# Moving the first batch's last stage into the second batch's attention, in one freed accumulation bank

## The reference

```python
def _L1_attn_ref(x, Wq, Wk, Wv, Wo, W_down_kv, W_up_k, W_up_v):
    ...
            scores = jnp.einsum('bhqd,bhkd->bhqk', qh, kh) * scale
            ...
            scores = scores * decay[None, None, :, :]
            ...
            attn = jax.nn.softmax(scores, axis=-1)
            out = jnp.einsum('bhqk,bhkd->bhqd', attn, vh)
            out = out.transpose(0, 2, 1, 3).reshape(B, S, D_MODEL)
            return (out @ Wo, latent_kv)
    ...
def _L1_ffn_ref(x, base_w, base_b, gate_w, lora_A, lora_B):
    ...
        logits = jnp.einsum('td,ed->te', xf, gate_w)
        probs = jax.nn.softmax(logits, axis=-1)
        weights, selected = jax.lax.top_k(probs, TOP_K)
        ...
        z = jnp.einsum('td,erd->ter', xf, lora_A)
        moe = jnp.einsum('ter,te,eor->to', z, ew, lora_B) * SCALING
        base = jnp.einsum('td,od->to', xf, base_w) + base_b
        out = (base + moe).reshape(x.shape[:-1] + (D_OUT,))
...
    x = x + _L1_attn_ref(_layernorm(x, axis=-1), L1_attn_Wq, ...)
    x = x + 0.5 * _L1_ffn_ref(_layernorm(x, axis=-1), L1_ffn_base_w, ...)
    return x
```

## Time and profile before

| | |
|---|---|
| median of 3 runs | 791.61 us (789.17 to 791.88) |
| the profiled execution | 787.95 us, its span 786.1 us |
| PE, DVE, ACT, POOL busy | 86%, 61%, 71%, 34% of the span |
| attention's exponentials | 466.8 to 728.2 us of the span |
| after the last exponential | 58.0 us |

### The profile page before, as it was taken

The page is one execution under the profiler, slowest core; times in us unless marked ns, Lnnn a source line. Parts: engine busy times, 40 slices in busy tenths (PEclk is TensorE's granted clock), DMA queues, the critical chain, the costliest instruction groups (busy, mean ns, idle before and its releaser), DMA issues.

```text
span 786.1 us, 11233 instructions
## 1 busy us (share of the span) xinstructions
PE 679.1 (86%) x3617; PEld 399.5 (51%) x3617; DVE 482.3 (61%) x1258; ACT 557.4 (71%) x789; POOL 271.2 (34%) x298
## 2 busy tenths in 40 slices
PE   3789788878889899999777769999999999999587
PEld 2566566656566667777555532332323223232364
DVE  4789877878798778988856552344322223222474
ACT  4657574666767666655453569999999999999243
POOL 3286456665667556455620430112000000000110
PEclk9999999999999999999958689999999999999858
DMA  9002232323223223333200189100199100000001
GB/s 261 11 1 70 80 97 80 90 84 91 86 82 97 90 84 115 102 124 114 73 15 0 27 179 194 31 1 1 20 187 196 29 1 1 1 1 1 3 1 54
DMA packets 31343, 54.55 MB, mean 69 GB/s; under 512 B 4624, under 2 KB 13280, under 8 KB 29776
## 3 DMA queue, kind: packets, MB, share of 16 engines
q1 hardware_dynamic: 30128, 53.38, 26.3%
q0 software_dynamic: 224, 0.34, 0.2%
q10 hardware_dynamic: 928, 0.06, 0.1%
HBM read 35.71 MB, written 1.28 MB: 47 GB/s over the span
## 4 chain that ended last, share of the span: by engine, by line
PE 33%; ACT 31%; issue 14%; DVE 13%; POOL 7%; ACTq 0%; DVEq 0%; POOLq 0%
ACT raw_w L836 26%; PE bank L1421 7%; PE bank L1423 6%; PE bank L1422 6%; POOL act_parts L576 4%; PE bank L1546 2%; PE bank L1543 2%; PE bank L1544 2%; PE bank L1461 2%; DVE act L1094 2%; DVE bank L1083 1%; POOL rstd L523 1%; DVE up L1072 1%; ACT xt L665 1%; PE bank L1476 1%
## 5 line engine op out<-in xcount | busy, mean ns | idle before, releaser
L836 ACT ACTIVATE raw_w<-bank,minus_c 128x1024 f32<-128x1024 f32 x256 | 259.6, 1165 | 1.8 <-PE bank L1722 0.7
L576 POOL TENSOR_TENSOR act_parts<-act,act_parts 128x512 fp32r<-128x512 f32 x128 | 167.4, 1309 | 120.6 <-ACT act_parts L737 99.9
L1266 DVE TENSOR_TENSOR bank<-bank,fix 128x256 f32<-128x256 f32 x128 | 55.3, 433 | 177.9 <-PE bank L1699 177.9
L723 ACT ACTIVATE bank<-bank,b_gate 128x512 f32<-128x512 f32 x112 | 74.1, 662 | 113.9 <-PE bank L1423 64.4
L1421 PE MATMUL bank<-xn_parts,w_hi 128*128 128x512 f32 x256 | 109.6, 428 | 20.1 <-ACT bank L723 10.2
L1072 DVE TENSOR_SCALAR up<-bank,b_up 128x512 f32<-128x512 f32 x128 | 95.5, 746 | 36.0 <-PE bank L1423 32.3
L1423 PE MATMUL bank<-xn_parts,w_hi 128*128 128x512 f32 x256 | 102.7, 401 | 0.0
L1422 PE MATMUL bank<-xn_parts,w_lo 128*128 128x512 f32 x256 | 102.4, 400 | 0.0
L520 POOL TENSOR_SCALAR var_eps<-mean_var 128x4 f32<-128x4 f32 x28 | 7.4, 263 | 236.2 <-DVE mean_var L940 234.9
L1094 DVE SCALAR_TENSOR_TENSOR act<-up,bank 128x512 f32<-128x512 f32 x128 | 86.6, 676 | 0.0
L737 ACT ACTIVATE act_parts<-act 128x512 fp32r<-128x512 f32 x128 | 79.8, 623 | 4.2 <-DVE act L1094 4.2
(11 more groups left out here) (204 smaller groups left out, 1057.6 us busy)
## 6 DMA issues: line engine op xcount, KB each, us to landing
grow<-scores SPq DMA_DIRECT2D x68, 256.0 KB, 3.2
early<-scores SPq DMA_DIRECT2D x44, 256.0 KB, 3.2
raw_w<-in_gate_up SPq DMA_DIRECT2D x4, 512.0 KB, 8.8
w_lo<-gelu_parts SPq DMA_DIRECT2D x8, 256.0 KB, 5.1
w_lo<-act_parts SPq DMA_DIRECT2D x8, 256.0 KB, 5.5
w_hi<-gelu_parts SPq DMA_DIRECT2D x6, 256.0 KB, 4.7
w_hi<-act_parts SPq DMA_DIRECT2D x6, 256.0 KB, 5.5
x_tok<-in_x SPq DMA_DIRECT2D x4, 256.0 KB, 4.4
```

The costliest lines, as they stand in the source:

```text
L576: pool.tensor_tensor(act_lo[:, j % NACT, :], act[:, j % NACT, :], act_hi[:, j % NACT, :].bitcast(F32), ALU.subtract).then_inc(s["lo_ready" ...
L723: eng.activation(out, bank[:, G, :], ACT.Gelu_apprx_sigmoid, bias=b_gate[:, e:e + 1]).then_inc(s["glu_ready"], 1)
L836: eng.activation(probs[:, u % NP, :], pair, ACT.Exp, bias=minus_c[:, b:b + 1])\
```

## The change

A table `EARLY` lays the whole remainder of chunks 0 and 1 (heads, projection, low-rank layer, turning back) into the steps of the second batch's attention: on PE at odd steps t from 69 to 125, behind `scores(2t + 1)`; on DVE at units u from 141 to 252, behind that unit's `fix_scores`. Of these chunks' work only the small router exponential stays on ACT (ahead of the exponentials of u = 190 and 201); the splits, scaled rows and copies that ACT did for all chunks are done by DVE for chunks 0 and 1. The stage "ffn1b" behind the attention begins with chunk 2 (`first=QC`).

The banks: from sum 8 on, all sums accumulate in bank 6 alone, so the first `weigh` of a sum waits until DVE has copied the sum before out; `take_out` moves from the sixth unit of the next sum to the fourth, `normalize` from the fourteenth to the tenth, `turn` from its sixth step to its fourth. Everything else (the turned sums and all 20 early steps of PE) shares bank 7, one after the other: `early_free` makes each wait for the reader of the one before.

```diff
+EARLY = {
+    "pe": {69: ("heads", 0), 71: ("heads", 1), 73: ("out", 0), 77: ("out", 1), 79: ("t1", 0), 85: ("t2", 0), 87: ("t1", 1),
...
+    "act": {190: ("exp", 0), 201: ("exp", 1)},
+}
...
+        def o_bank(n):
+
+            return 6 + n % 2 if n < G4 * QC else 6
...
+        turn_after = {KB // 2 * G4 * QC * 2 + KB * i + 3: ("turned", G4 * QC + i - 1) for i in range(G4 * QC)}
...
+                    if u in EARLY["act"]:
+                        router_exp(3, EARLY["act"][u][1])
...
-                    if u % (2 * KB) == 5 and n > 0:
+                    if u % (2 * KB) == (5 if u < UNITS else 3) and n > 0:
                         take_out(n - 1)
-                    if u % (2 * KB) == 13 and n > 0:
+                    if u % (2 * KB) == (13 if u < UNITS else 9) and n > 0:
                         normalize(n - 1)
+                    if u in EARLY["dve"]:
+                        early_step(*EARLY["dve"][u])
...
                     if i == 0 and n >= 2:
-                        pe.wait_ge(s["normed"], n - 1)
+                        pe.wait_ge(s["normed"], n - 1 if n <= G4 * QC else G4 * QC - 1)
+                    if i == 0 and n > G4 * QC:
+                        pe.wait_ge(s["ot_copied"], n)
...
-                    if t % KB == 5 and t >= KB:
+                    if t % KB == 5 and KB <= t < UNITS // 2:
                         turn(t // KB - 1)
+                    if t in turn_after:
+                        early_free("turned", turn_after[t][1])
+                        turn(turn_after[t][1])
+                    if t in EARLY["pe"]:
+                        name, c = EARLY["pe"][t]
+                        early_free(name, c)
+                        if name == "heads":
+                            pe.wait_ge(s["normed"], heads_whole(c))
+                        early_step(name, c)
...
+            def early_free(name, i):
+
+                at = early_uses.index((name, i)) if name != "last" else len(early_uses)
+                if at >= 1:
+                    signal, value = early_read(*early_uses[at - 1])
+                    pe.wait_ge(s[signal], value)
...
-            skewed("ffn1b", "pe", {**lora(LN_FFN1B, 3, X_ATTN), "turn": turn_back})
+            skewed("ffn1b", "pe", {**lora(LN_FFN1B, 3, X_ATTN), "turn": turn_back}, first=QC)
```

More of the change, by code:

```diff
@@ L360, in side, with skewed @@
                             chains[chain][name](c)
-        def skewed(phase, engine, ops, once={}):
+        def skewed(phase, engine, ops, once={}, first=0):
             stage, order = STAGES[phase], ORDERS[phase][engine]
-            for step in range(NC + max(stage.values())):
+            for step in range(first, NC + max(stage.values())):
                 if step in once:
@@ L369, in skewed @@
                 for name in order:
-                    if 0 <= step - stage[name] < NC:
+                    if first <= step - stage[name] < NC:
                         ops[name](step - stage[name])
@@ L856, in attention @@
                     attn_fast()
-                    for b in range(NB):
-                        attn_heads(b)
+                    attn_heads(1)
                 with eng.Else():
@@ L918, in _ @@
             attention()
-            skewed("ffn1b", "act", {**lora(LN_FFN1B, 3), "copy": out_copy})
+            skewed("ffn1b", "act", {**lora(LN_FFN1B, 3), "copy": out_copy}, first=QC)
         @block.vector
@@ new lines, in early_hi, with early_score_copy @@
+            def early_hi(c):
+                eng.wait_ge(s["t2_ready"], norm_at(LN_FFN1B, c) + 1)
+                eng.tensor_copy(xn_hi[:, chunk(c)], bank[:, t2_bank(LN_FFN1B, c), :]).then_inc(s["xn_hi_ready"], 1)
+            def early_score_copy(c):
+                eng.wait_ge(s["score_psum_ready"], 3 * NC + c + 1)
+                for g in range(G4):
+                    eng.wait_ge(s[f"stack{g}_loaded"], stacks_in(g, 1))
+                eng.tensor_copy(score_rows_of(3, c), bank[0:2 * TRUE1, scores_bank(3, c), :])\
+                    .then_inc(s["score_ready"], 1)
@@ L1357, in attn_out @@
                 for c in range(QC * b, QC * (b + 1)):
[L1358 to L1360 removed]
+                    attn_add(c)
             def attention():
@@ L1413, in _ @@
             attention()
-            skewed("ffn1b", "dve", lora(LN_FFN1B, 3))
+            skewed("ffn1b", "dve", lora(LN_FFN1B, 3), first=QC)
         @block.tensor
@@ L1729, in turn @@
                     for t in range(TPC):
-                        last = pe.transpose(bank[:, 6 + n % 2, 128 * t:128 * (t + 1)],
+                        last = pe.transpose(bank[:, turned_bank(n), 128 * t:128 * (t + 1)],
                                             out_t[:, n % 2, 128 * t:128 * (t + 1)], ident[:])
@@ L1796, in attention @@
                     pe.wait_ge(s["ao_ready"], 1)
-                    for c in range(NC):
+                    before = None
+                    for name, c in EARLY["pe"].values():
+                        if before:
+                            signal, value = early_read(*before)
+                            pe.wait_ge(s[signal], value)
+                        early_step(name, c)
+                        before = name, c
+                    for c in range(QC, NC):
                         head_in(c)
-                for b in range(NB):
-                    attn_out(b)
+                attn_out(1)
             pe.wait_ge(s["ident_loaded"], 16)
```

181 lines of the change are left out of this document (133 added, 48 removed).

## The result

The changed kernel takes **780.61 us** in the median of 4 runs (778.69 to 781.08), the kernel before, run beside it, 791.71 us (789.17 to 791.88). The ratio is 0.986, with a 95% interval from 0.984 to 0.989: some 11 us faster, where 4.5 were forecast. The profiled execution took 781.08 us, its span is 779.2 us. Two later rounds gave 0.989 (0.981 to 0.997) and 0.987 (0.984 to 0.990).

A forecast was written before the change was run, and what follows sets the result against it. ACT bounds the second batch's attention, chains the tail behind it. Attention +10.4 us (9.1 pieces, 0.4 router exponentials, 0.9 bank and `logits(1)`), tail -14.9, net -4.5: profiled execution 783.5, median 787.1 us; range 783 to 792.

The forecast's parts named there:

- What bounds the kernel: Second batch's attention: ACT full, 32.88 of 33.00 us; behind the attention no engine full, chains set the pace, mean clock 0.70.
- The slack of 0.30: Second batch's attention: `turn` takes 0.59 us of PE and ACT loses 0.29, so PE has 0.30 us free per inserted piece.
- I price it as its time on PE less 0.30: Early PE pieces in the second batch's attention: each costs ACT that much, 4.55 us a chunk, 9.1 for two.
- lower bound of 6 us: Second batch's attention: least growth, if half of each piece's price is made up for; 10.4 us was the forecast.
- The single bank: First `weigh` of sums 9, 11, 13, 15 waits for the copy: 0.5 us each, partly filled by early pieces, 0.8 in all.
- `logits(1)`'s wait: Second batch's attention: `logits(1)` waits for its split, 0.1 us.
- The router exponentials: Two small exponentials on the full ACT in the second batch's attention: 0.2 us each, 0.4 together.
- DVE's work at nothing: Second batch's attention: DVE's added 28 us for both chunks cost no time, since DVE is busy only 9.09 of 33 us.
- Rival 2: Attention: early DVE pieces wait for PE and delay corrections at ten places; at 1 us each 797.1 us, slower; chance 0.10.
- What the tail gives back: From the last exponential to the end: 43.15 us instead of 58.0, 14.9 less, walked step by step at half clock.
- Rival 3: Tail: the clock returns to full from `zs(3)` on, 2.3 us more gain, 784.8 us; chance 0.15.
- aside on another price for the transposes: Skill page's 56 ns per product: an insert of four costs about 0.07 us, ten of them 2.2 us less than forecast.

The follow-up runs named there:

- doubled transposes: Kernel before with `turn` at step 6, its four transposes done twice in a row there; against single transposes there, both batches' exponentials span 265.9 us, +6.7.
- half of the change: Changed kernel with the single accumulation bank and only chunk 0's steps early, chunk 1's left behind the attention; 787.2 us, 0.994 of the kernel before.
- single-bank kernel: Kernel before with every second-batch sum accumulating in bank 6 and turned into bank 7, no early pieces; second batch's exponentials span 131.3 us, before 129.1.

## Why the prediction was wrong, and where it was right

**What bounds the kernel** was right: ACT in the attention, chains behind it.

**The slack of 0.30** was right for a lone piece: `logits(1)` lost 0.67 of 1.00, the doubled transposes 0.73 of 1.02.

**The step that failed is "I price it as its time on PE less 0.30", for each of the 20 pieces by itself.** They stand two steps apart for the most part, and there the slack is 0.30 plus what the piece two steps ahead has cost. Priced by that rule, with the prediction's own times on PE (and 1.0 for `logits`), the steps from 67 to 125 give: `turn` 0.29, heads 0 and 0.29, projection 0.20, `turn` 0.09, projection 0.40, `t1` 0, `turn` 0.29, `t2` 0, and so on, 6.9 us in all with the turns. Measured were stalls of 7.5 us over the whole stretch. Of these 0.24 are the two router exponentials, 0.07 the bank, and 0.28 a delay on ACT ahead of one exponential (below); 6.9 are left. The turns alone had cost 2.34 before, so the pieces added 4.6 us, where the prediction had 9.1. The rule is not exact at single places: it gives 0.29 and then 0.20 for `scores(0)` and `z(0)`, and 0.04 and 0.51 were measured; `back(0)` cost 0.88 instead of 0.70. The errors cancel in the sum, and that they do so nearly exactly is in part luck.

The prediction's lower bound of 6 us, "if half of each piece's price is made up for", was the right idea without the reason, and even so too high.

**The single bank** was sized rightly, wait and cost (0.5 against 0.45, 0.8 in all against 0.7 alone). In the changed kernel it cost 0.07 in sum 11, and at sums 9, 13 and 15 nothing that can be told from the pieces there: here too the coupling takes it in, as half of the change shows (0.44 without a piece two steps ahead). The prediction added 0.9 for it and for `logits(1)`'s wait. **The router exponentials** cost 0.12 each, not 0.2.

**DVE's work at nothing** was right: DVE is busy 16.88 of 33 us, and each of the 20 exponentials of this stretch that start more than 0.05 us late stands behind a piece of PE, a router exponential or the first `weigh` of sum 11. Rival 2, the one on the slow side, didn't occur. At one place ACT was held up for longer than PE's piece explains, at unit 208 behind `z(0)`, by 0.79: `weigh` ends at 684.17 and the exponential starts at 684.58, 0.41 later, where it is 0.13 at the other large stalls. Its signals from PE had all come by 684.22, and it waits for none from DVE. The four other executions of this attention have the same 0.41. The cause of these 0.28 us stays open.

**What the tail gives back** was right step by step, to 0.3 us in each row above. The clock was at half from 741.6 to 748.4 us and again from 751.8 to 775.7; it was full in between, while PE stood idle, and for the last 3.4 us, behind a stretch in which PE had been busy throughout. Rival 3 took the clock's return from `zs(3)` on as a gain of 2.3 us, and it didn't return by itself before 775.7. Held at full through the whole tail on purpose, it gave 6.1.

**Net:** -9.2 us from the two stretches instead of -4.5, nearly all of the difference from the attention. The medians' 11 us have an interval from 9 to 13, and -9.2 lies at its near edge; that the rest is the variation ahead of the attention is not shown.

**The prediction's aside on another price for the transposes** enters no sum, but it is worked wrongly. The Trainium skill, "TensorE: Matmul & The Clock Gate", section "Back-to-back issue gap", has about 56 ns for one product; four of them are, as an estimate from it, 0.22 us and not 0.37. By the prediction's rule that is less than the slack of 0.30 and would cost nothing, and the ten inserts would be 2.9 us cheaper and not 2.2. In the trace four held PE for 0.58 to 0.59 us.

**The range** took 6 us as the least that the attention can pay, where 5.4 were measured, and went down to 783. With the measured -9.2 the median would have been 782.5, so the pricing of the pieces alone carries it out of the range. What would have shown it lies in the trace of before, right behind the earlier trace rows (timeline of PE):

```profile
690.35 1.04 PE L1722 MATMUL bank<-raw_w,act 128*9 128x512 f32 x8
...
691.96 1.05 PE L1722 MATMUL bank<-raw_w,act 128*9 128x512 f32 x8
...
693.79 0.49 PE L1699 MATMUL bank<-w_lo,score_t 32*128 32x512 f32 x2 [0.35 <-ACT raw_w L836]
```

The `weigh` after the stall's follows it in 1.61 us, not the 1.99 of a step: PE's own work for a step is only that. And 0.35 us stand idle ahead of 693.79, where PE waits for an exponential from behind the stall. I took ACT's loss from that place, and not PE's state after it.

## What to carry to other kernels

When work is laid into a stage that another engine bounds, ask after each piece where the engine that does it stands when the stall is over. If it waits on signals from ahead of the stall, and has a free step in which to make up its own time, it has gained a lead, and the next piece is cheap up to that lead. Here that was at a distance of two steps, with three pairs of banks between the engines; other distances and other depths of buffers were not tried. So pieces are best put in pairs at that distance, large with large: a pair costs about the larger one less the slack (shown for equal pieces of 0.59 us; for large ones only in the changed kernel, where `z(1)` and `back(0)` cost 0.54 and 0.88). At half the distance the pair cost more than both in full (6.3 us for 15 extra pieces, 4.35 at full price), at double the distance nearly that (3.5).

Where a tail of chains is left with the clock at half, price the clock by itself: products that nobody reads, put only where the engine waits and into a bank that nobody uses, took six of forty-three microseconds. With somewhat fewer of them the clock fell for the last 16 us, so read it after each try.

## What the runs showed of the hardware

In two executions the clock fell to half for 3.4 us inside the second batch's attention, with TensorE busy nearly all the time before. In the third run of the changed kernel, at 790.54 us the slowest of its seven, (windows, columns as above):

```profile
640.00:678.40 38.40, 37.35 (x280) 14.01 (x280) 20.29 (x72) 37.80 (x39) 3.40 (x8) 1.00 0.00 1
678.40:681.80 3.40, 3.40 (x22) 0.75 (x22) 0.77 (x2) 1.91 (x2) 0.00 (x0) 0.50 0.00 0
```

TensorE had been busy for 37.35 of the 38.4 us before, and its longest gap there was 0.42 us (in the single-bank kernel for 6.89 of the 7.9 us before, with a gap of 0.56). ACT lost 1.4 us by it over the batch (135.9 instead of 134.5), a quarter of what the change costs the attention; in the single-bank kernel 1.5. The Trainium skill, "TensorE: Matmul & The Clock Gate", section "What's actually happening", has the low clock follow from idleness; these rows don't agree. I can't say what the cause is.
